# Layer 0 attention: rows divided by their denominators between two block transposes on VectorE

## The reference, cut to what matters

```python
def _L0_attn_ref(hidden_states, ..., Wq, bq, Wk, bk, Wv, bv, Wo, bo, ln_scale, ln_bias):
    ...
    scores = jnp.einsum('bhqd,bhkd->bhqk', q, k) / scale
    ...
    scores = scores + (c2p + p2c) / scale
    probs = jax.nn.softmax(scores, axis=-1)
    ctx = jnp.einsum('bhqk,bhkd->bhqd', probs, v)
    ctx = jnp.transpose(ctx, (0, 2, 1, 3)).reshape(B, S, H)
    out = ctx @ Wo + bo + hidden_states
    ...
x = x + _L0_attn_ref(xn, ...) + _L0_ffn_ref(xn, L0_ffn_weight)
```

## Time and profile before

| | |
|---|---|
| median of 3 runs | 2039.35 us (2037.15 to 2039.51) |
| the profiled execution | 2040.11 us, with a span of 2038.3 us from first to last instruction |
| granted TensorE clock, mean | 0.969; 1.00 in layer 0 from 100 to 700 us |
| layer 0's loop of steps | from about 48 to 801 us of the span |
| busy share of the span | PE 92%, DVE 75%, ACT 73%, POOL 59% |

### The profile page before, as it was taken

The page is one execution under the profiler, slowest core; times in us unless marked ns, Lnnn a source line. Parts: engine busy times, 40 slices in busy tenths (PEclk is TensorE's granted clock), DMA queues, the critical chain, the costliest instruction groups (busy, mean ns, idle before and its releaser), DMA issues.

```text
span 2038.3 us, 38730 instructions
## 1 busy us (share of the span) xinstructions
PE 1884.0 (92%) x13494; PEld 1462.9 (72%) x13494; DVE 1519.4 (75%) x3871; ACT 1480.9 (73%) x2979; POOL 1197.3 (59%) x1027
## 2 busy tenths in 40 slices
PE   4899999999999996789998999999999888889998
PEld 3677777777777774555776887888877666668797
DVE  7677777877787874474388888888889777754686
ACT  6788888888888885334467677777776677785675
POOL 3888888898888873365255555555555444437200
PEclk7999999999999998699998999999999899999999
DMA  6999999999999982201000000000010000012001
GB/s 189 336 335 328 315 337 314 324 337 315 335 315 331 322 314 78 79 1 41 1 6 1 1 1 1 1 1 1 1 32 1 1 1 1 1 47 78 12 1 42
DMA packets 72263, 263.98 MB, mean 130 GB/s; under 512 B 10822, under 2 KB 30406, under 8 KB 71558
## 3 DMA queue, kind: packets, MB, share of 16 engines
q1 hardware_dynamic: 71126, 256.53, 36.6%
q10 hardware_dynamic: 944, 4.98, 0.6%
HBM read 140.17 MB, written 121.31 MB: 128 GB/s over the span
## 4 chain that ended last, share of the span: by engine, by line
PE 41%; DVE 7%; ACT 6%; POOL 2%; issue 2%; DVEq 0%; ACTq 0%; POOLq 0%
PE PS L157 10%; PE PS L339 8%; PE PS L161 8%; PE PS L163 7%; PE PS L162 7%; ACT AR L167 3%; ACT L167 2%; DVE AR L185 1%; DVE PT L181 1%; DVE DR L181 1%; ACT PT L171 1%; POOL AR L176 1%; DVE AR L176 1%; DVE AR L193 1%; POOL X L181 0%
## 5 line engine op out<-in xcount | busy, mean ns | idle before, releaser
L167 ACT ACTIVATE AR<-PS,AR 128x512 f32<-128x512 f32 x1024 | 699.8, 690 | 174.0 <-PE PS L339 79.1
L339 PE MATMUL PS<-ident,AR 128*128 128x128 f32 x3816 | 577.7, 276 | 33.2 <-DVE PT L181 19.3
L339 PEld LDWEIGHTS PS<-ident,AR 128*128 128x128 f32 x3816 | 445.8, 141 | 123.1 <-issue 46.0
L157 PE MATMUL PS<-AR 128*128 128x128 bf16 (+7 forms) x4126 | 483.7, 357 | 36.0 <-DVE AR L1393 13.8
L181 POOL TENSOR_TENSOR AR<-AR 128x512 f32<-128x512 f32 (+7 forms) x325 | 384.9, 1197 | 186.3 <-DVE AR L181 63.8
L207 DVE CUSTOM_DVE_ANT_0 PS<-PS,AR 128x512 f32<-128x512 f32 x512 | 353.4, 695 | 165.4 <-PE PS L587 160.8
L176 POOL TENSOR_SCALAR AR<-AR 128x512 f32<-128x512 f32 (+1 forms) x146 | 251.9, 1726 | 269.1 <-DVE AR L1797 200.3
L171 ACT ACTIVATE AR<-PS 128x512 f32<-128x512 f32 (+3 forms) x596 | 350.0, 589 | 49.8 <-PE PS L157 26.1
L157 PEld LDWEIGHTS PS<-AR 128*128 128x128 bf16 (+4 forms) x4126 | 291.1, 131 | 109.9 <-issue 60.8
L193 DVE TENSOR_REDUCE AR<-PS 128x1 f32<-128x512 f32 x384 | 263.5, 687 | 81.7 <-PE PS L163 75.2
L171 ACT ACTIVATE PT<-PS 128x512 fp32r<-128x512 f32 x320 | 191.4, 598 | 163.7 <-PE PS L339 130.7
(11 more groups left out here) (177 smaller groups left out, 3065.8 us busy)
## 6 DMA issues: line engine op xcount, KB each, us to landing
scr<-AR SPq DMA_DIRECT2D x128, 800.0 KB, 4.9
XN<-scr SPq DMA_DIRECT2D x85, 768.0 KB, 6.9
AR<-scr SPq DMA_DIRECT2D x43, 768.0 KB, 7.2
AR<-qsc SPq DMA_DIRECT2D x96, 192.0 KB
qsc<-AR SPq DMA_DIRECT2D x16, 384.0 KB, 4.5
qsc<-AR SPq DMA_DIRECT2D x16, 256.0 KB, 4.6
AR<-in_wgu SPq DMA_DIRECT2D x16, 256.0 KB, 3.0
qsc<-AR SPq DMA_DIRECT2D x16, 128.0 KB, 4.5
```

The lines of the kernel that those rows point to most:

```text
L157: return pe.e.matmul(out, lhsT, rhs, start=start, stop=stop)
L167: return ac.e.activation(out, in_, func, bias=bias, scale=scale, accum_out=accum)
L339: return pe.e.transpose(out, in_, ident[0:k, 0:k])
```

## The change

The four heads' sums are no longer copied by ACT and transposed by PE. VectorE reads bank `B_PV` itself with a transpose that works on blocks of 32x32. In `OS` each partition then holds, for every block, one token's eight channels and its denominator side by side. DVE takes the 16 reciprocals and multiplies, into `CT`, and after the fourth group a second block transpose brings `CT` to `CTT`, channels on partitions again. The channels arrive in another order, so the rows of `Wo` are laid out by it (on the host). The uses `heads` and `ct` of bank `B_M`, `os_out` and `ct_out` are gone, DVE's work on group G stands at its step 28 + 16G, where ACT's copy was, and the last sequence's chain is put at earlier steps.

```diff
-        CT = A0.take(4, 4, 4, 8)
-        RD = A0.take(4, 4)
+        CT = A0.take(16, 32)
+        RD = A0.take(16)
...
-        HEADS = (33, 47, 62)
-
-        ENDS = [{"heads": 17, "ct": 19, "mo": 29, "sw": 31, "stats": (34, 36, 38, 40), "var": 42, "root": 42, "scale": 46,
+
+        ENDS = [{"mo": 29, "sw": 31, "stats": (34, 36, 38, 40), "var": 42, "root": 42, "scale": 46,
...
-        ENDS += [{"heads": 14, "ct": 16, "mo": 18, "stats": (19, 19, 19, 19), "var": 19, "root": 19, "scale": 20, "norm": (20, 20, 20, 20),
-                  "sw": 19, "sum": 21, "last": (22, 22, 22, 22), "lastvar": 22}]
+        ENDS += [{"sw": 6, "mo": 13, "stats": (14, 14, 14, 14), "var": 14, "root": 14, "scale": 15, "norm": (15, 15, 15, 15),
+                  "sum": 16, "last": (17, 17, 17, 17), "lastvar": 17}]
...
-                elif what == "heads":
-                    pe.wait_ge(os_c, 4 * b + g + 1)
-                    for q in range(4):
-                        ins = tr(pe, ps[:, q * 128:q * 128 + 128], OS[:, q * 128:q * 128 + 128])
-                elif what == "ct":
-                    pe.wait_ge(*emptied[number["heads", b, 3]])
-                    for q in range(4):
-                        ins = tr(pe, ps[:, q * 128:q * 128 + 128], CT[:, q, :, :, :].rearrange("p g h d -> p (g h d)"))
                 elif what == "mo":
-                    pe.wait_ge(*emptied[number["ct", b, 0]])
+                    pe.wait_ge(ct_dv, b + 1)
...
-            def heads_out(b, g):
-                ps = PS[:, B_M, :].rearrange("p (q h r) -> p q h r", q=4, h=4)
-                dv.wait_ge(m_mm, number["heads", b, g] + 1)
+            def heads_out(G):
+
+                b, g = divmod(G, 4)
+                rows = OS.rearrange("p (i r) -> p i r", r=32)
+                dv.wait_ge(pv_mm, G + 1)
                 dv.settle()
-                dv.step(dv.e.reciprocal(RD, ps[:, :, :, 8]))
+                dv.e.transpose(OS, PS[:, B_PV, :]).then_inc(os_c, 1)
+                dv.wait_ge(os_c, G + 1)
+                dv.step(dv.e.reciprocal(RD, rows[:, :, 8]))
                 dv.settle()
                 if b and g == 0:
-                    dv.wait_ge(m_mm, number["ct", b - 1, 0] + 1)
-                tt(dv, CT[:, :, g, :, :], ps[:, :, :, 0:8], bc(RD.unsqueeze(3), [128, 4, 4, 8]), ALU.mult).then_inc(m_dv, 1)
+                    dv.wait_ge(ct_dv, b)
+                dv.step(tt(dv, CT[:, :, 8 * g:8 * g + 8], rows[:, :, 0:8], bc(RD.unsqueeze(2), [128, 16, 8]), ALU.mult))
+                if g == 3:
+                    dv.settle()
+                    dv.wait_ge(t1_ok, b)
+                    dv.e.transpose(CTT, flat(CT)).then_inc(ct_dv, 1)
...
-                if b < NB and r - 1 in HEADS:
-                    heads_out(b, HEADS.index(r - 1))
+                G, k = divmod(u - 28, 16)
+                if k == 0 and 0 <= G < 4 * NB:
+                    heads_out(G)
...
-            def os_out(G):
-                ac.wait_ge(pv_mm, G + 1)
-                if G:
-                    ac.wait_ge(m_mm, number["heads", (G - 1) // 4, (G - 1) % 4] + 1)
-                copy(ac, OS, PS[:, B_PV, :]).then_inc(os_c, 1)
-
-            def ct_out(b):
-                ac.wait_ge(m_mm, number["ct", b, 0] + 1)
-                ac.wait_ge(t1_ok, b)
-                copy(ac, CTT, PS[:, B_M, :]).then_inc(m_ac, 1)
...
-    d["l0_wv"], d["l0_wo"] = f["L0_attn_Wv"], f["L0_attn_Wo"]
+    by_place = np.arange(128).reshape(4, 4, 8).transpose(1, 0, 2).reshape(128)
+    d["l0_wv"], d["l0_wo"] = f["L0_attn_Wv"], f["L0_attn_Wo"][by_place]
```

More of the change, by code:

```diff
@@ L459, in small @@
             uses = []
-            if b >= 1 and r in (ENDS[b]["heads"], ENDS[b]["ct"], ENDS[b]["mo"], ENDS[b]["sw"]):
-                uses += [(k, b - 1, 3 if k == "heads" else 0) for k in ("heads", "ct", "mo", "sw") if ENDS[b][k] == r]
+            if b >= 1:
+                uses += [(k, b - 1) for k in ("mo", "sw") if ENDS[b][k] == r]
             if b + 1 < NB:
-                uses += [(k, b + 1, 0) for k, at in AHEAD.items() if r == at]
-            if b < NB and r in HEADS:
-                uses.append(("heads", b, HEADS.index(r)))
+                uses += [(k, b + 1) for k, at in AHEAD.items() if r == at]
             return uses
-        order = [(k, 0, 0) for k in ("q", "k", "v", "far", "g0")]
+        order = [(k, 0) for k in ("q", "k", "v", "far", "g0")]
         for u in range(STEPS0):
@@ L472, in program @@
             number[use] = i
-            if use[0] in ("q", "k", "far", "g0", "ct"):
+            if use[0] in ("q", "k", "far", "g0"):
                 n_ac += 1
@@ L494, in bank @@
             def bank(use):
-                what, b, _ = use
+                what, b = use
                 i = number[use]
@@ L501, in small_mm @@
             def small_mm(use):
-                what, b, g = use
+                what, b = use
                 ps = bank(use)
@@ L512, in small_mm @@
                 elif what == "g0":
-                    pe.wait_ge(*emptied[number["k", b, 0]])
+                    pe.wait_ge(*emptied[number["k", b]])
                     for x in range(2):
@@ L602, in pv @@
                     pe.wait_ge(to_a, 16 * G + 16)
-                    pe.wait_ge(*emptied[number["v", b, 0]])
+                    pe.wait_ge(*emptied[number["v", b]])
                     if G:
@@ L619, in l0_pe @@
             pe.wait_ge(n_xt, 1)
-            small_mm(("q", 0, 0))
-            small_mm(("k", 0, 0))
+            small_mm(("q", 0))
+            small_mm(("k", 0))
             norm_tr(pe, 0, 1, 4, 1)
             for what in ("v", "far", "g0"):
-                small_mm((what, 0, 0))
+                small_mm((what, 0))
             norm_tr(pe, 0, 2, 4, 2)
             norm_tr(pe, 0, 3, 4, 3)
-            pe.wait_ge(*emptied[number["g0", 0, 0]])
+            pe.wait_ge(*emptied[number["g0", 0]])
             pe.wait_ge(pg_r, 8 * 16)
@@ L636, in l0_pe @@
             pe.wait_ge(n_xt, 8)
-            pe.wait_ge(*emptied[number["v", 0, 0]])
+            pe.wait_ge(*emptied[number["v", 0]])
             for u in range(STEPS0):
@@ L727, in v_out @@
             def v_out(b):
-                dv.wait_ge(m_mm, number["v", b, 0] + 1)
+                dv.wait_ge(m_mm, number["v", b] + 1)
                 dv.wait_ge(po_init, VA_0)
@@ L781, in tail @@
                     if r == at["stats"][q]:
[L782 removed]
+                        dv.wait_ge(*emptied[number["mo", b]])
                         dv.step(dv.e.bn_stats(lst[:, q, :], T1[:, q, :]))
@@ L825, in l0_dv @@
                     at = ENDS[b]
-                    if r == at["heads"] + 1:
-                        heads_out(b - 1, 3)
                     if r == at["mo"] + 1:
@@ L858, in xf_out @@
                 ps, k = small_bank(what, b), ("q", "k", "far", "g0").index(what)
-                ac.wait_ge(m_mm, number[what, b, 0] + 1)
+                ac.wait_ge(m_mm, number[what, b] + 1)
                 ac.wait_ge(sp_p, 6 * b)
@@ L875, in split_ac @@
                 if half == 0:
-                    ac.wait_ge(*emptied[number[("q", "k", "far")[k], b, 0]])
+                    ac.wait_ge(*emptied[number[("q", "k", "far")[k], b]])
                     if b:
@@ L946, in l0_ac @@
                         split_ac(b + 1, k // 2, k % 2)
-                G, k = divmod(u - 28, 16)
-                if k == 0 and 0 <= G < 4 * NB:
-                    os_out(G)
                 if b >= 1:
-                    if r == ENDS[b]["ct"] + 1:
-                        ct_out(b - 1)
                     for q in range(4):
@@ L983, in corr @@
                 step = G0A[b % 2][:, x, :, h:h + 1]
-                po.wait_ge(*emptied[number["g0", b, 0]])
+                po.wait_ge(*emptied[number["g0", b]])
                 if n >= 1:
@@ L1014, in tail @@
                 po.settle()
-                po.wait_ge(*emptied[number["sw", b, 0]])
+                po.wait_ge(*emptied[number["sw", b]])
                 tt(po, X[:, xs, :], X[:, xs, :], T1, ALU.add).then_inc(t1_ok, 1)
```

13 lines of the change are left out of this document (6 added, 7 removed).

## The result

| | before | after |
|---|---|---|
| median of 10 runs each | 2039.43 us (2037.02 to 2042.41) | 2043.24 us (2038.28 to 2048.91) |
| ratio, 95% interval | | 1.0023 (1.0013 to 1.0033) |
| the profiled execution | 2040.11 us | 2048.03 us |

The change makes the kernel 3.8 us slower; 5.5 us faster had been forecast. The profiled execution of the changed kernel is one of its slower ones, 4.8 us above its median, so the traces stand 7.9 us apart, of which 3.8 are the medians' difference. The granted clock is 0.969 in both.

What follows compares the result with a forecast made beforehand. PE, busy 596 of 600 us, was first suspect, with ACT, DVE and POOL limiting what comes back. 3.0 + 2.5 + 1.8 - 0.8 - 2.1 + 1.1 = 5.5 us gained gave 2033.9 us, 8-in-10 range 2026 to 2045.

Steps and rivals of the forecast that it cites:

- r = 33, `heads`: Removing this PE transpose lets the `scores` of r = 36 start 0.37 us earlier, 8 times, 3.0 us gained.
- r = 17 and 19: Two PE uses less, but `scores` wait for ACT's `exp`: 0.36 of 0.86 us gained, 7 times, 2.5 us.
- r = 60 to 64: `least` comes 0.76 us late, mostly covered by ACT; `heads` at r = 62 still gains 0.22 us, 8 times, 1.8 us.
- r = 44 to 51: Late DVE still finds POOL blocking its Newton operation; `heads` at r = 47 gains nothing, 0.1 us lost 8 times, 0.8 us.
- r = 12 to 14: The multiply waits out POOL, so PE's `g_of` at r = 14 starts 0.3 us late, 7 times, 2.1 us lost.
- last group's chain: From ACT's copy to the first `mo` matmul, 3.38 us become 2.28, 1.1 us gained at the end.
- the sum for a group's work on DVE: Transpose 0.78 us, then reciprocal and multiply, 1.30 us in all ahead of `least` at r = 28, 44 and 60.
- Rival 3: Slower through DVE's late `least`, with a transpose of 1.2 us or more plus the wait: 2047 us, chance 0.15.
- Rival 2: Gains and losses cancel, POOL's operations meeting the multiply at r = 44 and 60 too: 2039 us, chance 0.20.
- The ceiling: 40 uses of 0.43 us taken from PE, 17.2 us at most if nothing else waited.
- Rival 1: PE's time comes back whole, 18.3 us gained with the last chain: 2021 us, chance 0.12.
- `sw` put earlier hides nothing more: At the end of the last sequence, moving `sw` ahead gains nothing, since its result is only due at the end.

Runs made afterwards that it cites:

- e1: Changed kernel with the reciprocals `RD` moved into PSUM columns of `B_PV`, so the multiply has one SBUF and one PSUM input; 2036.82 us, ratio 0.999 to the kernel before.
- e12: Changed kernel without division on DVE, and ACT's third-part copies at r = 17 and 20 cut from 512 to 32 columns; 2030.61 us, ratio 0.9951 to the kernel before.
- e2: Changed kernel without the division on DVE, small memsets in its place; 2031.23 us, ratio 0.9961 to the kernel before.
- e3: Changed kernel with `sw` put behind the last group again, at step 14 of the last stretch; 2043.84 us, ratio 1.0025 to the kernel before.
- e4: Changed kernel with reciprocal and multiply ten steps after the first transpose, second transpose twelve steps after; 2037.17 us, ratio 0.9989 to the kernel before.
- e7: e4 with the second group's multiply four steps later, the last two groups done at once and `sw` late; 2033.38 us, ratio 0.9967 to the kernel before.
- e13: e7 with the Newton steps, norms and the second half of each sequence's end moved later; 2027.39 us, ratio 0.9934 to the kernel before.

## Why the prediction was wrong

The sum had five parts with a sign each. In the loop, by the table of places:

| step of the forecast | forecast | changed kernel |
|---|---|---|
| r = 33, `heads` | 0.37 x 8 gained | 0.28 x 8 gained |
| r = 17 and 19 | 0.36 x 7 gained | 0.25 x 7 gained |
| r = 60 to 64 | 0.22 x 8 gained | 0.56 x 8 lost |
| r = 44 to 51 | 0.1 x 8 lost | 0.94 x 8 lost |
| r = 12 to 14 | 0.3 x 7 lost | 0.07 x 7 lost |
| last group's chain | 1.1 gained | 1.17 gained, 1.2 lost to `sw` |

The rows of the loop add up to 8.5 us lost; the loop lost 6.96, since the first and the last sequence lost less than the mean.

**The step that failed** is the sum for a group's work on DVE, 1.30 us, applied at r = 28, 44 and 60, with 0.29 us for the multiply in it. The forecast had the mechanism: it read in the earlier trace rows that a DVE operation with two SBUF inputs waits out POOL's, and charged this to the multiply at r = 12, where it looked for POOL's rows. At r = 44 and 60 it put the wait at nothing. It waits there as well (1.10 and 1.18 us at 397.56 and 421.53). In the mean of all 32 the work is 0.72 + 0.25 + 0.78, about 1.75 us, and in the second to the seventh sequence the multiply takes 0.92 us at r = 44 and 1.12 at r = 60, so about 1.9 and 2.1 us at the two places that count.

What the wait costs can be read off sequence by sequence, in the changed kernel's trace (second to seventh sequence):

| group done at | multiply, us | lost, us |
|---|---|---|
| r = 60 | 1.20, 1.18, 1.18, 1.20, 0.75, 1.19 | 0.64, 0.63, 0.63, 0.64, 0.20, 0.60 at r = 62 to 65 |
| r = 44 | 0.56, 0.63, 1.10, 1.35, 0.87, 1.00 | 0.10, 0.18, 0.65, 0.89, 0.41, 0.54 at r = 44 to 46 |
| r = 12 | 0.55, 0.41, 0.29, 0.73, 1.16, 0.77 | 0, 0, 0, 0, 0.38, 0 at r = 14 to 16 |

The longer the multiply, the more is lost, one for one, beyond a length of 0.55 us at r = 60, 0.46 at r = 44 and 0.77 at r = 12. At r = 60 the same line leads to the 0.27 gained in e1, where the multiply takes 0.29: nothing there covers a late `least`, and 0.27 is near the forecast's 0.22.

**The rivals.** Rival 3 had named the threshold and the price: "about 1.75 us for a group's work", at 2 us per 0.1. The experiments give 1.9 us per 0.1. They stand at 1.26 us of work (-4.75 us of loop) and 2.01 (+9.55); a line between them passes +4.6 at 1.75, where the profiled loop has +6.96 (and a median execution of the changed kernel, 4.8 us shorter, perhaps less than the line). So the price was about right, as far as one trace per kernel tells, and the duration wrong. Rival 3 was tied to a slow transpose when the wait was enough. Rival 2 named the wait at both places and gave it a half microsecond, the mean of all 32 (775 - 291 = 484 ns), but charged 0.3 to 0.4 a place; it came to 0.8. At these places the wait is longer than the mean: 0.63 us at r = 44 and 0.83 at r = 60.

**r = 44.** The forecast held that DVE, 0.76 us late, still finds POOL at work on the pair that blocks its Newton operation, "so here nothing is lost". This fell. Its row of the kernel before has 1.54 us for the four operations; in the changed kernel, in the same sequence:

```profile
400.41 1.27 DVE L185 SCALAR_TENSOR_TENSOR AR<-AR 128x4 f32<-128x4 f32 x4
```

Counted from the start of step 44, they start 1.26 us later in the mean over the second to the seventh sequence and meet less of POOL's work (1.41 us instead of 1.68), so they end 1.00 us later, and r = 44 to 52 lose 0.94. Without the wait in the multiply (e1) they start 0.64 us later and end 0.30 later, and 0.25 is lost: the forecast's 0.1 was low there too.

**r = 12** was priced too high, and by one occurrence. At that very place the multiply took 0.73 us, near the forecast's 0.8, and r = 14 to 16 lost nothing. So it was not so that nothing behind it could make it up: up to a multiply of 0.77 us PE's `g_of` doesn't notice, and only one of the six sequences was beyond. (The last sequence, outside this mean, lost 0.75 us at r = 14 to 16, but e1, without the wait, lost the same.) What the Trainium skill says in "SBUF — State Buffer" (§ SBUF: two separate sides), that DVE with two SBUF inputs and GpSimd lock each other out for a whole instruction, agrees with the trace: 1.18 us for the multiply beside POOL at 421.53, 0.29 where POOL was idle. What was wrong was to look up POOL's rows at one place of four.

**r = 33 and 17 to 20**: the cause held, the size was a quarter to a third off. At r = 17 to 21 e12 shows it for 0.40 of the missing 0.60: ACT's copies, not PE, set the pace. At r = 33 to 37 all kernels have the same -0.28, e2 too, so DVE has no part in the missing 0.15; that it is `exp` behind `p_out` on ACT is read from the earlier trace rows and not tested.

**The ceiling.** Rival 1 was set against rightly: with no division at all the kernel gets 7 to 8 us of 17.2. Removing work from PE, which is busy 99% of the window, brought less than half of it.

**The last chain**: "`sw` put earlier hides nothing more" was wrong the other way round. It was in the way of the last products, and took back what the shorter chain gave: from the last `scores` to the first transpose of layer 1 are 30.1 us, 29.8 before.

What stays open: why the changed kernel's runs spread over 10.6 us where those before spread over 5.4. One execution has sequences that lose 0.15 and others that lose 1.85 us, by how much of POOL's work the multiply meets. e3, with the same waits, spreads over 12.6 us in 12 runs, e1, without them, over 5.5 in 11. POOL's start follows DMA arrivals at some places, so that the waits make the spread is plausible; it was not tried. In e3 the chain is 1.2 us ahead at `mo` but only 0.85 at layer 1, and e4's end is 0.76 us longer than the changed kernel's; neither was followed.

## What to carry to other kernels

When an operation moves from PSUM inputs to two SBUF inputs on DVE, look up what POOL does at every place where it will run, not at one, and charge the wait wherever the two meet; a small operand kept in PSUM takes the wait away. Judge it by the places where nothing covers it, not by its mean over all places. Work added to an engine that others wait for is cheapest in steps where the bounding engine has its longest share (here those with `pv`): moving it there was worth 9.9 us in the medians, from the changed kernel to e7. Read for each place which engine is ready last once the suspect is faster: with PE 99% busy, over half of the work taken from it came to nothing. And before two traces are compared by one stretch, look at what that stretch follows; here it was the end of four small operations, which moved by 0.4 us from one trace to the next.

## What the runs showed of the hardware

- A multiply with two SBUF inputs ends some 0.15 us behind the POOL operation that it waits out. Which one that is depends on when it is ready. In the changed kernel's trace it was ready 0.27 us or more before the end of a POOL operation, with the next right behind, at 11 places, and went ahead of that next one every time, as here (DVE, POOL):

```profile
444.78 0.73 DVE L181 TENSOR_TENSOR AR<-XN,AR 128x128 f32<-128x128 f32 x1
...
444.30 2.23 POOL L181 TENSOR_TENSOR AR<-AR 128x512 f32<-128x512 f32 x2
```

- Ready within 0.1 us of the end, as at 421.53, it waited out the following one too at 7 places of 8 and took 1.13 to 1.20 us. Five of the eight at r = 60 did. The longest of the 32 took 1.35 us, one that met no POOL operation 0.29.
- This is no rule of turns: in e4 and e13 single multiplies waited out two and three POOL operations although ready 0.7 us before the end of the first (1.92 us at 452.04 in e4, 3.03 at 541.68 in e13). What decides is open.
- The width of the operation is no protection: this one reads 128 elements per partition.
- One input in PSUM removes it wholly: 287 ns in the mean of 32, with POOL busy beside it.
- The block transpose of 128x512 fp32 takes 717 ns from PSUM and 711 from SBUF to SBUF, as long as `least` of the same size (695).
